# Where the causal mask of a grouped attention is added: by a product on TensorE, or by VectorE in the pass that takes the row maxima

## The reference, cut to what matters

```
scores = jnp.einsum('bkgtd,bksd->bkgts', qg, k) * scale
causal = jnp.tril(jnp.ones((T, T), dtype=bool))
scores = jnp.where(causal, scores, -jnp.inf)
attn = jax.nn.softmax(scores, axis=-1)
out = jnp.einsum('bkgts,bksd->bkgtd', attn, v)
```

## Time and profile before

| | us |
|---|---|
| median of 3 runs | 1985.68 |
| lowest and highest of 3 runs | 1982.91, 1986.48 |
| span of the profiled execution | 1983.0 |
| busy in that span: PE, DVE, ACT, POOL | 1888.2, 1137.8, 857.5, 869.0 |
| mask products of this stage on PE, 256 times | 58.3 |
| row maxima of this stage on DVE, 256 times | 124.8 |
| exponentials of this stage on ACT, 256 times | 136.9 |

### The profile page before, as it was taken

How to read it: one execution, slowest core, us unless ns; L and a number is a source line. 1 busy time by engine, 2 the same in 40 slices (tenths; PEclk the granted TensorE clock), 3 DMA queues, 4 the chain that set the end, 5 groups by cost and what they waited for, 6 DMA issues and landing times.

```text
span 1983.0 us, 29838 instructions
## 1 busy us (share of the span) xinstructions
PE 1888.2 (95%) x11008; PEld 1287.0 (65%) x11008; DVE 1137.8 (57%) x2177; ACT 857.5 (43%) x1896; POOL 869.0 (44%) x1380
## 2 busy tenths in 40 slices
PE   6999989999999999999999899999999998999998
PEld 3544447888888888888887687864444454544455
DVE  5676467666666666666667324146555355566465
ACT  1565544444444444444444333324565402565441
POOL 2454326545555555555554444423444312343352
PEclk9999999999999999999999999999999999999999
DMA  6113000101010101000000324112223103111101
GB/s 216 42 34 111 2 11 1 54 1 54 1 54 5 50 11 44 18 37 25 30 32 2 112 94 167 48 36 62 66 57 100 33 1 81 34 34 44 51 10 43
DMA packets 46211, 94.61 MB, mean 48 GB/s; under 512 B 7689, under 2 KB 35721, under 8 KB 43145
## 3 DMA queue, kind: packets, MB, share of 16 engines
q1 hardware_dynamic: 43474, 90.34, 13.9%
q10 hardware_dynamic: 2592, 2.36, 0.5%
HBM read 61.68 MB, written 2.10 MB: 32 GB/s over the span
## 4 chain that ended last, share of the span: by engine, by line
PE 81%; DVE 10%; ACT 4%; issue 2%; DMA 1%; POOL 0%; ACTq 0%; PEld 0%; SPq 0%; PEldq 0%; POOLq 0%; DVEq 0%
PE PS L1444 10%; PE PS L1544 9%; PE PS L463 6%; PE PS L566 6%; PE PS L1960 5%; PE PS L544 5%; PE PS L510 5%; PE PS L591 4%; PE PS L1522 3%; PE PS L1973 3%; PE PS L1506 3%; PE PS L1473 3%; PE PS L478 2%; PE PS L1931 2%; PE PS L512 2%
## 5 line engine op out<-in xcount | busy, mean ns | idle before, releaser
L990 ACT ACTIVATE PB<-PS 128x512 f32<-128x512 f32 x480 | 280.8, 599 | 236.2 <-PE PS L544 233.2
L897 POOL TENSOR_SCALAR_AFFINE_SELECT PB<-PB 128x256 f32<-128x256 f32 (+1 forms) x480 | 173.3, 365 | 319.7 <-ACT PB L990 313.6
L769 DVE TENSOR_REDUCE NM<-PS 128x2 f32<-128x1024 f32 x192 | 209.2, 1091 | 168.0 <-PE PS L512 166.6
L510 PE MATMUL PS<-KQ 96*128 96x512 bf16 (+3 forms) x768 | 184.7, 306 | 18.1 <-DVE NM L769 11.2
L544 PE MATMUL PS<-KQ 99*128 99x512 bf16 (+3 forms) x768 | 183.3, 304 | 4.7 <-ACT PB L990 3.4
L1727 ACT CAST OTH<-PS 128x512 fp32r<-128x512 f32 x64 | 37.5, 586 | 323.6 <-PE PS L1527 323.6
L1856 POOL TENSOR_SCALAR PR<-PR,RCP 128x512 f32<-128x512 f32 (+3 forms) x256 | 134.4, 534 | 95.3 <-DVE RCP L1655 95.0
L1667 DVE TENSOR_REDUCE NX<-PS 128x1 f32<-128x512 f32 (+3 forms) x256 | 124.8, 487 | 67.4 <-PE PS L1495 61.5
L463 PE MATMUL PS<-XTT,WA 128*128 128x512 f32 x288 | 144.8, 609 | 13.4 <-DVE ident_masks_b L2595 12.0
L512 PE MATMUL PS<-ident_masks_b 128*128 128x128 bf16 x768 | 149.0, 223 | 0.0
L1791 ACT ACTIVATE PR<-PS,NX 128x512 f32<-128x512 f32 (+3 forms) x256 | 136.9, 535 | 26.6 <-DVE NX L1667 21.6
(11 more groups left out here) (331 smaller groups left out, 4613.3 us busy)
## 6 DMA issues: line engine op xcount, KB each, us to landing
KQ<-HI SPq DMA_DIRECT2D x90, 128.0 KB, 2.4
KQ<-MID SPq DMA_DIRECT2D x72, 128.0 KB, 2.4
WB<-f_w SPq DMA_DIRECT2D x12, 768.0 KB, 4.4
WB<-w1o SPq DMA_DIRECT2D x8, 1024.0 KB, 8.0
WC<-f_w SPq DMA_DIRECT2D x10, 768.0 KB, 4.3
WB<-w1a SPq DMA_DIRECT2D x8, 768.0 KB, 4.3
WB<-w1b SPq DMA_DIRECT2D x8, 768.0 KB, 6.0
WA<-w SPq DMA_DIRECT2D x6, 1024.0 KB, 6.3
```

The lines of the kernel that those rows point to most:

```text
L510: pe.matmul(ps, KQ[0:SR, self.query(G, h), i * P:(i + 1) * P], KQ[0:SR, self.key(G, h), 0:n], start=True, stop=False)
L769: x = dve.tensor_reduce(nm[:, h:h + 2, i], PS[:, b:b + 2, 0:(i + 1) * P], AX.X, ALU.max, negate=True)
L897: pool.affine_select(blocks, blocks, [[0, count], [1, P]], ALU.is_ge, 0.0, base=0, channel_multiplier=-1).then_inc(s16["probs_ready"].sem, 1)
L990: act.activation(PB[:, n % PBS, :], PS[:, 4 + n % 2, :], ACT.Exp, scale=self.scale)\
```

## The change

TensorE no longer issues the mask products; the last matmul of a step's scores signals `scores`. A table CAUSAL (128x512: 384 columns of zeros, then the triangle with -1e30 above the diagonal) is loaded into SBUF. VectorE's `tensor_reduce` gives way to one `tensor_tensor_reduce` (`mask`): it reads the scores in PSUM and the last w columns of CAUSAL, writes -(scores + mask) to PR in SBUF, and keeps the row minimum of what it writes, which is the negated maximum, in NX. ScalarE's exponential reads and writes PR in place, with a scale of -1. The bank of a step is free as soon as VectorE is done (`negmax`, where `exp` stood). The wait for the transposes of head n-2 (they read the same slot of PR) moves from ScalarE to VectorE. The rotary passes wait for CAUSAL too.

```diff
@@ Attention1.scores (TensorE)
                 if m >= 2:
-                    pe.wait_ge(s1["exp"].sem, m - 1)
+                    pe.wait_ge(s1["negmax"].sem, m - 1)
...
-                    pe.matmul(ps, qL[:, n % 3, rows], kH[:, u % 2, keys], start=False, stop=False)
+                    x = pe.matmul(ps, qL[:, n % 3, rows], kH[:, u % 2, keys], start=False, stop=True)
                 else:
-                    pe.matmul(ps, qF[:, n % 3, :], kF[:, u % 2, :], start=True, stop=False)
-                pe.matmul(ps[:, w - P:w], identb[:, :], mask_qk[:, :], start=False, stop=True)\
-                  .then_inc(s1["scores"].sem, 1)
+                    x = pe.matmul(ps, qF[:, n % 3, :], kF[:, u % 2, :], start=True, stop=True)
+                x.then_inc(s1["scores"].sem, 1)
@@ VectorE
+            def mask(self, dve, n, i):
+
+                w, at = (NT - i) * P, OFF[NT - 1 - i]
+                if i == 0 and n >= 2:
+                    dve.wait_ge(s1["pT_psum"].sem, 4 * (n - 1))
+                dve.wait_ge(s1["scores"].sem, 4 * n + i + 1)
+                dve.tensor_tensor_reduce(PR[:, n % 2, at:at + w], PS[:, 2 + i % 2, 0:w], CAUSAL[:, T - w:T], -1.0,
+                                         -MASKED, ALU.add, ALU.min, NX[:, n % 2, i:i + 1])\
+                   .then_inc(s1["negmax"].sem, 1)
...
-                        dve.wait_ge(s1["scores"].sem, 4 * n + i + 1)
-                        dve.tensor_reduce(NX[:, n % 2, i:i + 1], PS[:, 2 + i % 2, 0:(NT - i) * P],
-                                          AX.X, ALU.max, negate=True).then_inc(s1["negmax"].sem, 1)
+                        self.mask(dve, n, i)
@@ ScalarE
-                        if i == 0 and n >= 2:
-                            act.wait_ge(s1["pT_psum"].sem, 4 * (n - 1))
                         act.wait_ge(s1["negmax"].sem, 4 * n + i + 1)
-                        act.activation(PR[:, n % 2, at:at + w], PS[:, 2 + i % 2, 0:w],
-                                       ACT.Exp, bias=NX[:, n % 2, i:i + 1],
+                        act.activation(PR[:, n % 2, at:at + w], PR[:, n % 2, at:at + w],
+                                       ACT.Exp, scale=-1.0, bias=NX[:, n % 2, i:i + 1],
                                        accum_out=SM[:, n % 2, i:i + 1]).then_inc(s1["exp"].sem, 1)
@@ SyncE, behind the first stage
             sp.dma_start(TAB[:, :, :], d["c_rope1"]).then_inc(s1_tab.sem, 16)
+            sp.dma_start(CAUSAL[:, :], d["c_causal"]).then_inc(s1_tab.sem, 16)
```

More of the change, by code:

```diff
@@ L333, in build @@
         Wo1L = sb("Wo1L", [P, GQ, D], F32R, L1)
+        CAUSAL = sb("CAUSAL", [P, T], F32, L1)
         L1.close()
@@ L1401, in vector @@
                 dve.wait_ge(self.tails[1].s_x.sem, self.tails[1].s_x.at(NT))
-                dve.wait_ge(s1_tab.sem, 16)
+                dve.wait_ge(s1_tab.sem, 32)
                 a1.rope(dve, 0)
@@ L2668, in tables @@
     c["c_ident_masks"] = np.stack([eye, m, m.T], 1)
+    c["c_causal"] = np.concatenate([np.zeros((P, T - P), f), m], 1)
     c["c_iota8"] = np.tile(np.arange(8, dtype=f), (P, 1))
```

## The result

The changed kernel takes 1967.47 us (median of 3 runs, 1966.90 to 1969.41) against 1984.30 (median of 4, lowest 1982.74): a ratio of 0.9918, interval 0.9902 to 0.9934, so 16 to 17 us faster. A fourth run of it, at a granted clock of 0.813 where the others show 0.981 to 0.983, took 2184.99 us and is left out of these figures (the median of all four is 1968.44 us). Forecast were 1969 us and a range of 1963 to 1984. The profiled execution has a span of 1965.2 us (1983.0 before) at the same mean clock, 0.982 against 0.983 of full speed.

A forecast was written before the change was run, and what follows sets the result against it. The prediction took TensorE to bound the kernel, busy 198.97 of 200 us in the stage. Each unit saves 0.78 + 0.29 = 1.07 us, times 16 is 17.1, taking the median from 1985.68 to 1969 us; range 1963 to 1984.

The forecast's parts named there:

- What bounds the stage: TensorE, busy 198.97 of 200 us in the stage; a freed slot moves everything behind it if no other engine is late.
- The slots, 0.26 us per head: TensorE loses 256 mask products, 0.07 us at three steps and 0.05 at step 3: 16.6 us over 64 heads.
- the rival that the slot isn't freed: Rival: weight loads or a semaphore hold the transposes, so the slot stays; within 2 us of before, 1985; 4%.
- VectorE's pass, e = 0.13: e is the new VectorE pass's extra cost with its read-out, over the reduction: between 0.07 and 0.31 us, taken as 0.13.
- h = 2, the bank wait turns into one for PTL: TensorE's 0.26 us wait at step 2 goes, but transposes then wait for step 0's PTL; 0.29 us saved with step 3's product.
- h = 1, VL: The output product needs VL, which VectorE delays by 3e (e: extra pass cost); stall 3e - 0.47, none at e = 0.13.
- h = 0 and 3: The last PTH on ScalarE comes later through VectorE's maxima; stall 2e - 0.35 (e: extra pass cost), none at 0.13.
- ScalarE, 0.03 us per exponential: Exponentials read SBUF instead of PSUM, 0.03 us more each, 8 us in all on an engine idle over half the stage.
- The sum: Per unit 0.78 us from three heads plus 0.29 at h = 2, 1.07 us; times 16 units, 17.1 us saved.
- The waits didn't move to VectorE's chains: Rival: extra pass cost of 0.17 to 0.3 us makes TensorE wait for VectorE; saving 14 to 0 us, middle 1977; 20%.
- Waits didn't all go: Rival: every TensorE wait on ScalarE goes too, PTL of step 0 being earlier than reckoned; 22.5 us saved, 1963; 8%.
- The slow pass: Rival: VectorE's new instruction takes two cycles per element or some tenths of a us fixed; 1999 or 2018 us; 10%.

The follow-up runs named there:

- Experiment 1: The kernel before with only the 256 mask products left out, so the mask is missing from the result: 1971.49 us, 0.9935 of the kernel before.
- experiment 4: The changed kernel with VectorE's L1644 at h = 2 moved from ahead of step 0's PTL to behind step 2's maxima: 1960.68 us.
- experiment 6: The changed kernel with an unread VectorE maximum over 8 elements of CAUSAL added behind every masking pass: 1970.22 us.
- experiment 7: The changed kernel with an unread VectorE maximum over 192 elements added behind every masking pass: 1987.19 us.
- experiment 8: The changed kernel with the masking pass split into an addition writing SBUF and a reduction that waits for it and reads it: 2052.62 us.
- experiment 3: The changed kernel with scores waiting again for the exponential of the step two before, instead of the maxima: 1972.69 us.

## Why the prediction was right, point by point

**What bounds the stage: right.** TensorE at 198.57 of 200 us after, and the freed slots came out as time.

**The slots, 0.26 us per head: right.** Experiment 1 has 0.26 to 0.28 us in the three heads where nothing else holds TensorE. The row duration of 0.23 us would have given 59 us over 256 products, and the rival that the slot isn't freed falls.

**VectorE's pass, e = 0.13: too dear, e is about 0.01.** The pass takes 692 ns like the reduction, and not the 751 ns of the three-operand pass. The read-out shows 83 ns and costs next to nothing, as VectorE's timeline at h = 1 shows:

```profile
747.81 0.69 DVE L1659 CUSTOM_DVE_ANT_0 PR<-PS,CAUSAL 128x512 f32<-128x512 f32 x1 [0.29 <-PE PS L1493]
748.43 0.08 DVE L1659 DVE_READ_ACCUMULATOR2_ANT NX<- 128x1 f32 x1
748.43 0.69 DVE L1644 TENSOR_TENSOR OTL<-PS,OTH 128x512 fp32r<-128x512 f32 x1
...
751.58 0.54 DVE L1638 TENSOR_TENSOR VL<-PS,VH 128x384 fp32r<-128x384 f32 x1
```

The next instruction starts at the read-out's own start, 0.62 us behind the pass; it was 0.61 behind the reduction. From step 0 to VL VectorE needs 3.77 us, against 3.78 before, three read-outs and all. The reciprocal of one element was the wrong neighbour for this price, and both of my bounds (0.07 and 0.31) lay above the truth. The rule of the Trainium skill that I weighed ("VectorE: DVE Perf Modes", "The DRAIN you can't avoid") would, by the sentence that I took from it, have made the read-out cost its whole duration, 0.08 us in the new trace, and the trace doesn't bear that out. The same paragraph goes on: "A next op that is not held starts earlier". I had left this out, and it is what this trace shows.

**h = 2, the bank wait turns into one for PTL: right, in size too, by two errors that cancel.** After, around step 2 of a head whose first scores start at 720.28:

```profile
723.82 0.55 DVE L1623 TENSOR_TENSOR PTL<-PS,PTH 128x384 fp32r<-128x384 f32 x1
...
724.51 0.41 PE L1506 MATMUL PS<-ident_masks,PR 128*128 128x128 f32 x2 [0.36 <-DVE PTL L1623]
```

The transposes start 4.23 us behind the first scores, 4.47 before. That is 0.24 saved; with step 3's product the head is 0.29 us shorter, just what the sum had. In this the right size is luck. But PTL's end at 724.37 and the transposes' start are 0.14 us apart, where I had put 0.03 for the signalling. So 0.12 of e that wasn't there paid for 0.11 of signalling that was. The row calls the wait 0.36 us, counted from the end of the matmul ahead, so of 0.1 to 0.3 as forecast it is a little over. What it costs is more: the transposes start 0.63 us behind L1493's start at 723.88, where unheld ones (experiment 4, 718.15 to 718.26) follow after 0.11. So 0.52 us are lost there. Experiment 4 takes the wait away and gains 0.40, since step 3's transpose then waits for PTL of step 1 and stands 0.34 us behind L1495, not 0.22 (719.18 to 719.52, against 725.46 to 725.68).

**h = 1, VL: right that there is no stall, wrong in the slack.** I wrote that the first scores are there 0.07 us sooner for VectorE. They aren't. Before, the pass started 0.27 us behind the start of the mask product (807.63 to 807.90) and 0.96 behind the first score matmul; now it starts 0.53 behind the start of the last full matmul and 1.00 behind the first:

```profile
746.81 0.40 PE L1491 MATMUL PS<-kH,qH 128*128 128x512 f32 x1
...
747.28 0.39 PE L1493 MATMUL PS<-kH,qL 128*128 128x512 f32 x1
747.50 0.60 PE L1506 MATMUL PS<-ident_masks,PR 128*128 128x128 f32 x4
```

The large last product holds VectorE longer than the small one did. So VectorE starts 0.04 later and not 0.07 sooner, and VL (ready at 752.12) stands 0.36 us ahead of the output product at 752.48, of which 0.14 is needed for the signal: 0.22 of slack by these rows where I had 0.47. The experiments make it smaller still: 0.21 us of pads cost 0.08 in experiment 6, and 0.81 us of them 0.66 in experiment 7, so the slack is about 0.14. With e near 0 nothing came of it. With a dearer pass it would have: the prediction's sum loses everything at e = 0.3, the one with these slacks at about 0.2.

**h = 0 and 3: no stall, right.** The last PTH ends at 744.51 + 0.27 = 744.78 and the product that needs it starts at 745.01. The list of waits has 4 for PTH in the whole stage, 3 of them in the last heads (2.4 of 2.8 us); before there were 3, 1.6 us. The prediction names waits for PTH as a sign that its step about VectorE is wrong; between 420 and 1042 us, in the steady units, there is none.

**ScalarE, 0.03 us per exponential: right** (734 against 701 ns), and hidden.

**The sum: 17.1 us forecast, 16.7 measured in the stage, 17.8 on the spans.** Per unit it is 1.08 us against 1.07. In the 14 whole units that is 15.2 against 15.0, and in the six heads ahead of the first output product 1.7 against 1.6. The last two heads, which I had counted like any others (0.29 + 0.26 = 0.55) with their loss set at nothing, lose 0.2 instead: 0.8 us off, where I had allowed 0.5. TensorE waits there for PTL four times (2.7 us) and for PTH three times (2.4 us). That the spans come out above the forecast all the same is luck: 1.2 us lie ahead of the stage, in code that is the same but for one load. In the ten traces the first scores start anywhere from 315.8 to 320.9 us, and TensorE's granted clock there is low at different times in each: from 274 to 280 us it is 0.61 before, 0.84 after and 1.00 in experiment 4. So I take the 1.2 us for the difference of two executions.

**The rivals.** The waits didn't move to VectorE's chains beyond PTL, because e is small. Waits didn't all go, because PTL stands behind the bank. The slow pass didn't happen; experiments 7 and 8 show that it would have eaten the gain through the waits, and earlier than described. The other reading of them, that VectorE's free time hides it all, is wrong by 16 x 1.26 = 20 and 16 x 5.18 = 83 us.

What the prediction had no term for is step 3 at h = 2, whose transposes come 0.22 us behind their scores after, but 0.31 to 0.34 in experiments 1, 3, 4 and 7 and 0.63 in experiment 8. Where VectorE is late or the wait at step 2 is gone, they wait for PTL of step 1: they start 0.14 us behind its end in experiments 4 (719.38 to 719.52), 7 (736.31 to 736.45) and 8 (770.46 to 770.60). Where the exponential frees the bank, it holds the scores of step 3, whose weight load waits for it for 0.25 us in experiment 1 and 0.33 us in experiment 3. What stays open is why the slack at h = 1 is 0.14 us where the rows say 0.22.

## What to carry to other kernels

A small instruction on the bound engine is worth its distance from start to start, not its row's duration. A slot freed ahead of a wait goes to the wait: look for what releases it, move that release, and then ask what is late next. Here that was one instruction of VectorE standing ahead of PTL, and moving it gave another 0.40 us per unit, more than a third of the whole change. How much more work a half idle engine may take is read from the slack of the chains by which the bound engine waits for it, not from its free time: here about 0.24 us per pass (an estimate between two measured points) would have taken the whole gain, on an engine that was then still 29% idle.

## What the runs showed of the hardware

- A VectorE pass that adds an SBUF source to a PSUM source, writes SBUF and keeps a minimum takes 692, 549, 419 and 285 ns for 512, 384, 256 and 128 elements. The plain reduction of experiment 1, which reads PSUM alone, takes 692, 548, 418 and 284.
- Its read-out shows 83 ns, and the next instruction starts together with it (both at 748.43). A reduction of 8 elements takes 0.07 us from its start to the next, one of 192 elements 0.27.
- From VectorE's end to the start of the matmul that waited for it pass 0.14 us (724.37 to 724.51, 714.67 to 714.81, 719.38 to 719.52 and 770.46 to 770.60).
- TensorE's granted clock fell in the last head but one in the kernel before and in the changed one (0.57 and 0.59 as the mean of 4 us, so for most of them at the lower of its two levels, 1.2 GHz). In the changed kernel that head took 1.3 us longer than in experiment 4, where the clock stayed at 1.00 behind a wait just as long.
- An exponential over 512 elements takes 734 ns from SBUF and 701 ns from PSUM; ScalarE's read-out behind it 190 against 202 ns.
- VectorE, waiting for the last matmul of a group, started 0.27 us behind the start of a last one of 128 columns in bf16, and 0.53 us behind the start of one of 512 columns in float32.
